# Mixer of an adaLN block: order of the copies behind a step's attention, one maximum per step, and the place of a kept copy of h

## The chip, the cores and the metric

One Trainium2 chip, one of its cores. The time is the device time of one execution in microseconds (us): the median over the runs shown. TensorE is PE here (its weight loads PEld), VectorE is DVE, ScalarE is ACT, GpSimd is POOL, and SP issues most of the DMAs.

## What is computed

The block runs an attention-and-scan stage over 16 sequences of 512 tokens of width 256, then an MLP, then a mixture of 8 experts. The change lies in the first stage, the "mixer". Cut to it:

```python
h = _layernorm(x, axis=-1) * (1 + ca) + sa          # modulated input, kept for the residual
xn = _layernorm(h, ln1_g, ln1_b)                    # second norm, of h
scores = einsum('bhncd,bhnkd->bhnck', Qb, Kw) / sqrt(Dh)
scores = where(mask, scores, -inf)                  # window of 64 queries, band of 128 keys
p = softmax(scores); o = einsum('bhnck,bhnkd->bhncd', p, Vw)
attn = o @ W_O + b_O
drive = xn @ B_w + u;  s2 = A * s + ut              # scan over the tokens
x1 = h + g * attn + (1.0 - g) * y_ssm
```

## The kernel before

The mixer is a loop over 16 batches, `body(b, last)` on each engine. The first and the last batch are written out, the 14 between them are a hardware loop. Engines are ordered by semaphores alone; each engine runs its own list in program order.

A batch begins with the projections (PE L129 to L131; the helper's lines). Then come 11 steps (`for s in steps`), a software pipeline over the 8 windows of 64 queries. In step s PE does, in this order:

- `scores_by_query(b, s)`: the scores of window s with queries on the partitions, into `sc[:, 0:2, :]` (L631, L636). They serve only to find each query's maximum.
- `scores_by_key(b, s-1)`: the scores of window s-1 again, with keys on the partitions, minus the maxima (L650, L658, L662). It waits for `maxT_sb`, the maxima turned onto a row and copied to `w["shift"]`.
- `values(b, s-2)`: probabilities times V, into `pv` (L672). It waits for `o_norm` of the window before.
- the turning of the maxima of window s (L734, into `pm`), then the turning of the normalised output of window s-3 (L744).

DVE does in step s: the two `tensor_reduce` (L887) of window s, one for each half of `sc`; in step 1 the scan (L899, L902); `layer_norms(dve, b + 1, s)`, which is a part of the two norms of the NEXT batch (step 0: statistics of x, which waits for the loads of x and of its modulation rows `shsc`; 1: aggregate; 2: normalise; 5: statistics of h; 6: aggregate; 7: normalise); then the reciprocal and the normalising of window s-2 (L908, L912), which wait for `pv_mm`; then the copy of the turned maxima (L917), which waits for `maxT_mm`; then the low half of the output (L921).

POOL refines the inverse roots of these norms by twelve small operations each (L101 to L104), computes h of the next batch (L989, L992) and the residual sum x1 (L1008). Before it overwrites `h` it waits for `h_kept`: that `h` of the batch before has been copied to `hres` by a DMA (L541).

In step 8 PE turns the next batch's normalised x (`transpose_x`, L569), which waits for step 7's normalising, and begins the output projections (`outputs`). `outputs(b, 0)` waits for all eight copies of maxima, since it writes the bank `pm` in which they are turned.

SP's list in a batch: four copies of K (L526), the load of the next x and `shsc` (L515, L520), in batch 0 alone `start.store_rest` (waits for the gates' modulation, which DVE computes in step 3 of batch 0) and `start.store_blanks` (L219, L236, L239), then the store of the gate rows to `scratch["xs"]` (L538), then the copy of h to `hres` (L541), then the store of x1 (L543).

Of the kernel before, what the change touches and what calls it, by code (L numbers as in the profile page):

```python
# [19 lines left out]
ALU = mybir.AluOpType  # L20
ACT = mybir.ActivationFunctionType
AX = mybir.AxisListType
# [11 lines left out]
WIN = 64  # L34
NW = L // WIN
# [361 lines left out]
def mixer(nc, din, w, scratch, out, NB):  # L397


    with ExitStack() as ctx:  # L400
# [68 lines left out]
        st_hi = m.counter("st_hi", 1)  # L469
        st_lo = m.counter("st_lo", 1)  # L470
        q_scores = m.counter("q_scores", 2 * NW)
        maxed = m.counter("maxed", 2 * NW)
        maxT_mm = m.counter("maxT_mm", NW)
        maxT_sb = m.counter("maxT_sb", NW)
        k_scores = m.counter("k_scores", NW)
# [32 lines left out]
        @block.sync  # L508
        def _(sp):
            def load(b):  # L510
                load_x(b)
                load_modulation(b)

            def load_x(b):
                sp.dma_start(x[:], din["x"][bass.ds(b, 1), :, :].rearrange("a (t p) d -> p (a t) d", p=P)  # L515
                             ).then_inc(x_in.sem, 16)

            def load_modulation(b):
                row = scratch["mod"][bass.ds(b, 1), 0:2 * D].rearrange("a (i d) -> a i d", i=2)
                sp.dma_start(shsc[:], row.to_broadcast([P, 2, D])).then_inc(x_in.sem, 16)  # L520

            def body(b, last):
                sp.wait_ge(k_lo.sem, k_lo.at(b, 2))
                for j in range(4):
                    r = slice(32 * j, 32 * j + 32)
                    sp.dma_start(Kz[r, j % 2, :, :, WIN:], Kt[r, :, :, :]).then_inc(k_spread.sem, 16)  # L526
                if isinstance(b, int) and b == 0:
                    start.store_bias_rows(sp)
                if not last:
                    sp.wait_ge(s_norm0.sem, s_norm0.at(b, 4))  # L530
                    sp.wait_ge(s_h.sem, s_h.at(b, 2))
                    load(b + 1)
                if isinstance(b, int) and b == 0:
                    start.store_rest(sp)
                    sp.wait_ge(start.mod_out.sem, 32)
                    start.store_blanks(sp)
                gate = scratch["mod"][bass.ds(b, 1), 5 * D:6 * D].to_broadcast([L, D])
                sp.dma_start(scratch["xs"][bass.ds(b * L, L), D:2 * D], gate).then_inc(gate_out.sem, 16)  # L538
                sp.wait_ge(s_h.sem, s_h.at(b, 2))
                sp.wait_ge(x1_sb.sem, x1_sb.at(b, 0))  # L540
                sp.dma_start(hres[:], h[:]).then_inc(h_kept.sem, 16)  # L541
                sp.wait_ge(x1_sb.sem, x1_sb.at(b, TT))
                sp.dma_start(scratch["x1"][bass.ds(b, 1), :, :].rearrange("a (t p) d -> p (a t) d", p=P),  # L543
                             x1[:]).then_inc(x1_out.sem, 16)

            load_x(0)
            start.load_job(sp, 0)
            start.load_vectors(sp)
            for j in range(1, len(start.jobs)):
                start.load_job(sp, j)  # L550
            start.store_shift_and_scale(sp)
            sp.wait_ge(start.mod_out.sem, 16)
            load_modulation(0)
            start.copy_constants(sp)
            loop(sp, body)
            sp.wait_ge(x1_out.sem, 16 * NB)
            sp.wait_ge(start.blank_out.sem, 48)
            sp.wait_ge(start.v_in.sem, 16 * 7)
            sp.wait_ge(gate_out.sem, 16 * NB)

        @block.tensor
        def _(pe):
# [59 lines left out]
            def scores_by_query(b, n):  # L622

                var = 1 if n == 0 else 0
                if n == 0:
                    pe.wait_ge(q_lo.sem, q_lo.at(b, 4))
                else:
                    pe.wait_ge(maxed.sem, maxed.at(b, 2 * n))
                for h in range(2):
                    r = half_rows(h)  # L630
                    pe.matmul(sc[:, h, :], w["twoI"][r, :], w["maskq"][r, var, :, :], start=True, stop=False)  # L631
# [74 lines left out]
            def body(b, last):  # L706
                project(b)
                for s in steps:
# [21 lines left out]
                    if 0 <= s - 2 < NW:  # L730
                        values(b, s - 2)
                    if s < NW:
                        pe.wait_ge(maxed.sem, maxed.at(b, 2 * s + 2))
                        pe.transpose(maxT, mx[:, s % 2, :], w["identb"][:]).then_inc(maxT_mm.sem, 1)  # L734
                    if s == NW + 1:
                        outputs(b, 1)
# [117 lines left out]
        def _(dve):  # L854
# [17 lines left out]
            def body(b, last):  # L872
# [9 lines left out]
                                      ).then_inc(k_lo.sem, 1)  # L882
                for s in steps:
                    if s < NW:
                        for c in range(2):
                            dve.wait_ge(q_scores.sem, q_scores.at(b, 2 * s + c + 1))
                            dve.tensor_reduce(mx[:, s % 2, WIN * c:WIN * c + 4],  # L887
                                              sc[:, c, :].rearrange("p (j k) -> p j k", j=4),
                                              AX.X, ALU.max).then_inc(maxed.sem, 1)
                    if isinstance(b, int) and b == 0 and s == 0:  # L890
                        for j in range(3, 6):
                            start.low_part(dve, j, start.low)
# [9 lines left out]
                        dve.tensor_copy(sth[:], st[:]).then_inc(st_hi.sem, 1)  # L902
                    if not last:
                        layer_norms(dve, b + 1, s)
                    if 0 <= s - 2 < NW:
                        n = s - 2
                        dve.wait_ge(pv_mm.sem, pv_mm.at(b, n + 1))
# [2 lines left out]
                        for par in range(2):  # L910
# [1 line left out]
                            dve.tensor_tensor(on[r, n % 2, :, :], pvO[r, :, DH * par:DH * par + DH],  # L912
                                              rden[r, n % 2, :].unsqueeze(2).to_broadcast([WIN, PAIRS, DH]),
                                              ALU.mult).then_inc(o_norm.sem, 1)
                    if s < NW:
                        dve.wait_ge(maxT_mm.sem, maxT_mm.at(b, s + 1))
                        dve.tensor_copy(w["shift"][:, s % 2, :], maxT).then_inc(maxT_sb.sem, 1)  # L917
                    if 0 <= s - 3 < NW:
                        n = s - 3
                        dve.wait_ge(oT_hi.sem, oT_hi.at(b, n + 1))  # L920
# [1095 lines left out]
```

## Time and profile before

| | us |
|---|---|
| median of 3 runs | 2383.28 |
| lowest and highest | 2371.1, 2385.2 |
| the profiled execution, device time | 2362.23 |
| its span, first to last instruction | 2360.1 |
| mixer: batch 0's first step to the last x1 | about 54 to 1160 |
| PE busy over the span | 1995.8 (85%) |
| DVE busy over the span | 1429.3 (61%) |
| mean granted TensorE clock | 0.898 |

The mixer takes nearly half of the span. The profiled execution is 21 us below the median of the runs shown. A timeline row gives start, duration (or the stretch that merged instructions cover), engine, line, operation, output and inputs, the count, and in brackets the idle time of the engine before it with what ended it.

### The profile page before, as it was taken

The numbers are of one execution on the slowest core, as the hardware profiler recorded it, in microseconds if no ns is written. First come the engines' busy times: TensorE is split into PE (matmuls) and PEld (weight loads), VectorE is DVE, ScalarE is ACT, GpSimd is POOL, SyncE is SP. The second block draws the span as 40 slices with busy tenths as digits, with TensorE's granted clock in tenths as the row PEclk, the third lists the DMA queues.
The fourth block names the chain that finished last, engine by engine and source line by source line (L and its number), as shares of the span: only waits on it lengthen the run. The fifth ranks groups of instructions, "written<-read, shape, count | busy, mean of one in ns | idle before, by whom it ended". The sixth has DMA issues, their size and how long they took to land. (4 is left out here: it accounts for less than half of the span.)

```text
span 2360.1 us, 58051 instructions
## 1 busy us (share of the span) xinstructions
PE 1995.8 (85%) x19628; PEld 1589.9 (67%) x19629; DVE 1429.3 (61%) x3705; ACT 961.8 (41%) x1734; POOL 993.9 (42%) x1131
## 2 busy tenths in 40 slices
PE   4488988888889888889698988888089999999997
PEld 1366767666667666667556666666078888888886
DVE  5345454555555555554378888888345566666665
ACT  3133222233333323233165444455055565656564
POOL 3121121212112212222046766777446666666664
PEclk7689797998899999998799888889589999999999
DMA  3112001111110111111144333333135444554544
GB/s 121 54 50 50 18 31 49 49 49 49 49 36 23 39 49 49 49 49 36 47 131 134 119 115 117 119 125 121 37 86 91 88 91 92 94 90 89 92 92 61
DMA packets 155521, 172.90 MB, mean 73 GB/s; under 512 B 35141, under 2 KB 136200, under 8 KB 155329
## 3 DMA queue, kind: packets, MB, share of 16 engines
q1 hardware_dynamic: 101248, 96.90, 14.9%
q0 software_dynamic: 36352, 56.78, 12.9%
q10 hardware_dynamic: 17856, 18.37, 2.2%
q8 instruction: 40, 0.66, 0.1%
q14 instruction: 25, 0.20, 0.0%
HBM read 109.40 MB, written 53.99 MB: 69 GB/s over the span
## 5 line engine op out<-in xcount | busy, mean ns | idle before, releaser
L1878 POOL DMA_INDIRECT out<-experts_y,experts_entry x144 | 237.4, 1649 | 192.9 <-DVE experts_y L1854 165.9
L672 PE MATMUL mixer_pv<-w_V,mixer_prob 128*128 128x33 f32 x2048 | 271.7, 290 | 14.3 <-DVE mixer_on L912 14.3
L672 PEld LDWEIGHTS mixer_pv<-w_V,mixer_prob 128*128 128x128 f32 x2048 | 259.1, 205 | 28.2 <-issue 19.2
L799 ACT ACTIVATE mixer_prob<-mixer_sc 128x1024 f32<-128x1024 f32 x128 | 130.9, 1023 | 236.1 <-PE mixer_sc L662 236.1
L887 DVE TENSOR_REDUCE w_mx<-mixer_sc 128x4 bf16<-128x512 f32 x256 | 163.8, 681 | 90.4 <-PE mixer_sc L636 90.4
L1819 DVE TENSOR_SCALAR experts_v<-experts_v 128x512 f32<-128x512 f32 x144 | 74.6, 518 | 218.8 <-ACT experts_v L1793 218.8
L1793 ACT ACTIVATE experts_g<-experts_pg,x_b 128x256 f32<-128x256 f32 x288 | 120.9, 471 | 183.1 <-PE experts_pv L131 183.0
L1868 POOL DMA_INDIRECT experts_rows<-scratch_xs,experts_entry x144 | 168.7, 1171 | 59.4 <-issue 42.4
L1008 POOL TENSOR_TENSOR mixer_x<-mixer_mix,mixer_hres 128x256 f32<-128x256 f32 x64 | 46.5, 726 | 333.2 <-DVE mixer_mix L868 332.2
L129 PE MATMUL experts_pg<-experts_xT,x_w 128*128 128x256 f16 x576 | 158.1, 274 | 11.3 <-issue 8.7
L908 DVE RECIPROCAL mixer_rden<-mixer_pv 128x8 f32<-128x8 f32 x128 | 26.4, 207 | 232.1 <-PE mixer_pv L672 232.1
L1493 POOL DMA_INDIRECT scratch_queue<-mlp_entry,mlp_slot x128 | 142.2, 1111 | 50.9 <-issue 38.6
L129 PE MATMUL experts_py<-x_w,experts_hh 128*128 x576 | 157.7, 274 | 2.1 <-DVE experts_hl L1831 2.1
L131 PE MATMUL experts_py<-x_w,experts_hl 128*128 x576 | 157.8, 274 | 0.0
L130 PE MATMUL experts_py<-x_w,experts_hh 128*128 x576 | 157.7, 274 | 0.0
L131 PE MATMUL experts_pg<-experts_xT,x_w 128*128 128x256 f16 x576 | 157.6, 274 | 0.0
L130 PE MATMUL experts_pg<-experts_xT,x_w 128*128 128x256 f16 x576 | 157.6, 274 | 0.0
L129 PE MATMUL experts_pv<-experts_xT,x_w 128*128 128x256 f16 x576 | 157.5, 273 | 0.0
L131 PE MATMUL experts_pv<-experts_xT,x_w 128*128 128x256 f16 x576 | 157.4, 273 | 0.0
L130 PE MATMUL experts_pv<-experts_xT,x_w 128*128 128x256 f16 x576 | 157.4, 273 | 0.0
L650 PE MATMUL mixer_sc<-w_twoI,w_maskq 64*128 64x512 bf16 x256 | 55.2, 427 | 115.4 <-DVE w_shift L917 98.0
L662 PE MATMUL mixer_sc<-mixer_Qh,w_Kz 64*128 64x128 f16 x2048 | 150.1, 236 | 0.0
(364 smaller groups left out, 6022.3 us busy)
## 6 DMA issues: line engine op xcount, KB each, us to landing
mixer_x<-in_x SPq DMA_DIRECT2D x16, 512.0 KB, 3.9
w_Kz<-mixer_Kt SPq DMA_DIRECT2D x64, 128.0 KB, 2.4
scratch_xs<-scratch_mod SPq DMA_DIRECT2D x16, 512.0 KB, 10.0
mixer_hres<-mixer_h SPq DMA_DIRECT2D x16, 512.0 KB, 10.4
scratch_x<-mixer_x SPq DMA_DIRECT2D x16, 512.0 KB, 2.9
mlp_xa<-scratch_x SPq DMA_DIRECT2D x16, 512.0 KB, 4.3
mlp_stage<-in_x_w SPq DMA_DIRECT2D x16, 512.0 KB, 4.3
mlp_xb<-scratch_x SPq DMA_DIRECT2D x16, 512.0 KB
```

What stands on the lines that cost most here:

```text
L129: pe.matmul(out, lhs[0], rhs[0], start=start, stop=False)
L130: pe.matmul(out, lhs[0], rhs[1], start=False, stop=False)
L131: return pe.matmul(out, lhs[1], rhs[0], start=False, stop=stop)
L662: last = pe.matmul(sc[:, 2 + h, at:at + P], Kz[half_rows(h), j, i, c, keys], queries(q, h, c, n), start=False, stop=(c + j == 2 and i == 1))
L672: last = pe.matmul(pvO[:, i, :], prob[:, n % 2, at:at + P], V[:, n, i, :], start=True, stop=True)
L799: act.activation(prob[:, n % 2, :].rearrange("p (c j) -> p c j", c=2), sc[:, 2:4, :], ACT.Exp, scale=SCALE).then_inc(exped.sem, 1)
L887: dve.tensor_reduce(mx[:, s % 2, WIN * c:WIN * c + 4], sc[:, c, :].rearrange("p (j k) -> p j k", j=4), AX.X, ALU.max).then_inc(maxed.sem, 1)
L1493: pool.indirect_dma_start(out=scratch["queue"], out_offset=bass.IndirectOffsetOnAxis(ap=slot[:, 2 * t + k:2 * t + k + 1], axis=0), in_=ent ...
L1793: act.activation(dst[:, q, f * ROWS:(f + 1) * ROWS], bank[:, q, f * ROWS:(f + 1) * ROWS], fn, bias=x["b1"][:, bass.ds(e, 1), bias + 2 * q ...
L1819: dve.tensor_scalar(v[:, q, :], v[:, q, :], -8.0, 10.0, ALU.max, ALU.min).then_inc(v_cut.sem, 1)
L1868: pool.indirect_dma_start(out=rows[:, s, t, :], out_offset=None, in_=scratch["xs"], in_offset=bass.IndirectOffsetOnAxis(ap=entry[:, s, t, ...
L1878: pool.indirect_dma_start(out=out, out_offset=bass.IndirectOffsetOnAxis(ap=entry[:, s, t, 0:1].bitcast(I32), axis=0), in_=y[:, s % 2, t, : ...
```

## The change

Four edits, all in the mixer.

1. One `tensor_reduce` over both halves of `sc` (128 x 1024 elements to 128 x 8) takes the place of two (128 x 512 to 128 x 4). It waits for both score counts; `maxed` counts one per step.
2. The copy of the turned maxima (L917) goes ahead of the reciprocal and the normalising. It stays behind the norms and the scan of its step.
3. On SP the copy of h to `hres` goes ahead of batch 0's start-up stores and of the gate store.
4. PE's waits on `maxed` follow the new count.

```diff
-        maxed = m.counter("maxed", 2 * NW)
+        maxed = m.counter("maxed", NW)
...
                     load(b + 1)
+                sp.wait_ge(s_h.sem, s_h.at(b, 2))
+                sp.wait_ge(x1_sb.sem, x1_sb.at(b, 0))
+                sp.dma_start(hres[:], h[:]).then_inc(h_kept.sem, 16)
                 if isinstance(b, int) and b == 0:
                     start.store_rest(sp)
                     sp.wait_ge(start.mod_out.sem, 32)
                     start.store_blanks(sp)
                 gate = scratch["mod"][bass.ds(b, 1), 5 * D:6 * D].to_broadcast([L, D])
                 sp.dma_start(scratch["xs"][bass.ds(b * L, L), D:2 * D], gate).then_inc(gate_out.sem, 16)
-                sp.wait_ge(s_h.sem, s_h.at(b, 2))
-                sp.wait_ge(x1_sb.sem, x1_sb.at(b, 0))
-                sp.dma_start(hres[:], h[:]).then_inc(h_kept.sem, 16)
...
-                    pe.wait_ge(maxed.sem, maxed.at(b, 2 * n))
+                    pe.wait_ge(maxed.sem, maxed.at(b, n))
...
-                        pe.wait_ge(maxed.sem, maxed.at(b, 2 * s + 2))
+                        pe.wait_ge(maxed.sem, maxed.at(b, s + 1))
...
-                        for c in range(2):
-                            dve.wait_ge(q_scores.sem, q_scores.at(b, 2 * s + c + 1))
-                            dve.tensor_reduce(mx[:, s % 2, WIN * c:WIN * c + 4],
-                                              sc[:, c, :].rearrange("p (j k) -> p j k", j=4),
-                                              AX.X, ALU.max).then_inc(maxed.sem, 1)
+                        dve.wait_ge(q_scores.sem, q_scores.at(b, 2 * s + 2))
+                        dve.tensor_reduce(mx[:, s % 2, :].rearrange("p (h r) -> p h r", h=2)[:, :, 0:4],
+                                          sc[:, 0:2, :].rearrange("p h (j k) -> p h j k", j=4),
+                                          AX.X, ALU.max).then_inc(maxed.sem, 1)
...
                         layer_norms(dve, b + 1, s)
+                    if s < NW:
+                        dve.wait_ge(maxT_mm.sem, maxT_mm.at(b, s + 1))
+                        dve.tensor_copy(w["shift"][:, s % 2, :], maxT).then_inc(maxT_sb.sem, 1)
                     if 0 <= s - 2 < NW:
...
-                    if s < NW:
-                        dve.wait_ge(maxT_mm.sem, maxT_mm.at(b, s + 1))
-                        dve.tensor_copy(w["shift"][:, s % 2, :], maxT).then_inc(maxT_sb.sem, 1)
                     if 0 <= s - 3 < NW:
```

## Rows read from the trace of the kernel before

**Rows 1.** The page's costliest groups: count, busy, mean ns, idle before and releaser.

```profile
L887 DVE TENSOR_REDUCE w_mx<-mixer_sc 128x4 bf16<-128x512 f32 x256 | 163.8, 681 | 90.4 <-PE mixer_sc L636 90.4
...
L650 PE MATMUL mixer_sc<-w_twoI,w_maskq 64*128 64x512 bf16 x256 | 55.2, 427 | 115.4 <-DVE w_shift L917 98.0
```

**Rows 2.** Timeline of PE, batch 9: steps 1 and 3, then step 3 into 4.

```profile
707.90 0.61 PE L650 MATMUL mixer_sc<-w_twoI,w_maskq 64*128 64x512 bf16 x2 [2.73 <-DVE w_shift L917]
...
719.80 0.39 PE L650 MATMUL mixer_sc<-w_twoI,w_maskq 64*128 64x512 bf16 x2 [0.60 <-DVE w_shift L917]
...
722.82 0.22 PE L734 MATMUL mixer_pm<-w_identb,w_mx 128*128 128x128 bf16 x1
...
723.32 0.39 PE L636 MATMUL mixer_sc<-w_Kz,mixer_Qh 64*128 64x128 f16 x8
724.19 0.39 PE L650 MATMUL mixer_sc<-w_twoI,w_maskq 64*128 64x512 bf16 x2 [0.48 <-DVE w_shift L917]
```

**Rows 3.** Timeline of PE, batch 2, at half clock: two steps without that wait.

```profile
252.99 0.64 PE L636 MATMUL mixer_sc<-w_Kz,mixer_Qh 64*128 64x128 f16 x8
253.54 0.61 PE L650 MATMUL mixer_sc<-w_twoI,w_maskq 64*128 64x512 bf16 x2
...
260.61 0.61 PE L650 MATMUL mixer_sc<-w_twoI,w_maskq 64*128 64x512 bf16 x2
```

**Rows 4.** Timeline of DVE, batch 9, steps 3 to 7.

```profile
723.02 0.21 DVE L908 RECIPROCAL mixer_rden<-mixer_pv 128x8 f32<-128x8 f32 x1 [2.09 <-PE mixer_pv L672]
...
723.91 0.23 DVE L917 COPY w_shift<-mixer_pm 128x128 bf16<-128x128 bf16 x1
...
724.37 1.28 DVE L887 TENSOR_REDUCE w_mx<-mixer_sc 128x4 bf16<-128x512 f32 x2
...
729.96 1.39 DVE L820 BATCH_NORM_STATS2 mixer_stats<-mixer_h 128x6 f32<-128x256 f32 x4
...
733.15 1.28 DVE L887 TENSOR_REDUCE w_mx<-mixer_sc 128x4 bf16<-128x512 f32 x2
...
735.15 0.17 DVE L94 TENSOR_SCALAR mixer_rs<-mixer_rs 128x4 int32<-128x4 int32 x1
...
739.85 1.38 DVE L832 TENSOR_SCALAR mixer_nrm<-mixer_h,mixer_mv,mixer_rs 128x256 f32<-128x256 f32 x4 [1.03 <-POOL mixer_rs L104]
```

**Rows 5.** Timeline of PE, batch 9, start of step 8.

```profile
741.36 1.59 PE L569 MATMUL mixer_sc<-w_identf,mixer_nrm 128*128 128x128 f32 x8 [0.65 <-DVE mixer_nrm L832]
```

**Rows 6.** Timeline of SP, batch 0: its DMA issues.

```profile
57.25 0.51 SPq L520 DMA_DIRECT2D mixer_shsc<-scratch_mod  x1
79.14 0.34 SPq L219 DMA_DIRECT2D scratch_mod<-setup_mod  x1
...
89.69 11.54 SPq L541 DMA_DIRECT2D mixer_hres<-mixer_h  x1
```

**Rows 7.** The same batch on POOL, DVE and PE.

```profile
108.38 2.34 POOL L989 TENSOR_TENSOR mixer_h<-mixer_nrm,mixer_shsc 128x1024 f32<-128x1024 f32 x1 [36.11 <-DMA mixer_hres<-mixer_h]
...
113.17 1.40 DVE L820 BATCH_NORM_STATS2 mixer_stats<-mixer_h 128x6 f32<-128x256 f32 x4 [24.46 <-POOL mixer_h L992]
...
115.64 0.61 PE L650 MATMUL mixer_sc<-w_twoI,w_maskq 64*128 64x512 bf16 x2 [23.30 <-DVE w_shift L917]
...
126.49 1.04 PE L569 MATMUL mixer_sc<-w_identf,mixer_nrm 128*128 128x128 f32 x8
```

**Rows 8.** Timeline of PE, last batch, start of step 8.

```profile
1142.52 0.27 PE L129 MATMUL mixer_pm<-w_c_hi,mixer_sth 128*128 128x256 f16 x1 [1.12 <-DVE w_shift L917]
```

**Rows 9.** DMA issues of 700 to 716 us: count, KB, us to landing.

```profile
mixer_hres<-mixer_h SPq DMA_DIRECT2D x1, 512.0 KB, 10.6
mixer_shsc<-scratch_mod SPq DMA_DIRECT2D x1, 256.0 KB, 4.9
```

**Rows 10.** Stretches: length, busy time and count of each engine, PEclk, DMA share, GB/s.

```profile
741.00:747.00 6.00, 5.64 (x58) 4.47 (x58) 1.44 (x6) 2.80 (x6) 0.00 (x0) 0.72 0.00 0
246.00:270.00 24.00, 23.52 (x199) 20.15 (x193) 11.70 (x40) 6.12 (x10) 2.38 (x12) 0.52 0.00 0
```

## Prediction

> **What bounds the kernel now.** I read the page first: how busy each engine is, the granted clock along the span, and the costliest groups. In the mixer the slices show PE at 80 to 90%, with DVE at half and ACT and POOL below, so PE sets the pace and what counts is the time it stands. The group of L650, the first matmul of `scores_by_key`, is where it stands: 98.0 us of idle time, all released by the copy of the maxima, L917 [rows 1]. The list of PE's waits gives 87 such waits. The timeline of PE sorts them. In batch 0 one is 23.30 us [rows 7]. Step 1 of each later batch waits 1.7 to 3.2 us (2.73 in [rows 2]; 7.5 in batch 0). Step 3 waits 0.60 and steps 4 to 7 wait 0.48 each [rows 2], wherever PE is at full clock. At half clock there is no wait: L650 follows the scores at once [rows 3].
>
> The timeline of DVE says why. In step 3 the reciprocal starts at 723.02, when the values are done; the copy comes last at 723.91, though PE had turned the maxima at 722.82 + 0.22 = 723.04 [rows 2, 4]. PE stands until 724.19 for a copy of 0.23 us that two other operations delay by 0.89 us.
>
> **The copy ahead of the normalising.** DVE stands idle for 1.8 to 2.1 us before the values of steps 3 and 4 end [rows 4], so it is free when the turned maxima come. The copy then runs from about 723.09 to 723.32. Before, L650 started 0.05 after the copy's end (724.14, 724.19), so it could go at 723.37. PE's own order lets it go later: the modelled end of the last score matmul is 724.19 - 0.48 = 723.71, and at half clock L650 starts 0.09 before that modelled end (252.99 + 0.64 = 253.63, start 253.54) [rows 3]. At full clock I take 0.06, hence 723.65. The gain is 0.48 + 0.06 = 0.54 us in a step and 0.60 + 0.06 = 0.66 in step 3; the bounds are 0.48 and 0.6 for the one, 0.60 and 0.7 for the other. The period of a step goes from 4.39 (719.80 to 724.19) to 3.85.
>
> What is behind the copy on DVE? The reciprocal starts 0.3 us later and the reduction only 0.05 later (724.42), since the same operations have changed places. PE asks for the normalised output only a step later. The maxima of that reduction are wanted at the next turning, 722.16 + 3.85 = 726.0; they are there at 725.7 at the latest. Nothing new waits there.
>
> Step 5 is tighter. Its statistics of h end at 729.96 + 1.39 = 731.35 [rows 4] and move with the turning of step 4, by 0.66 + 0.54 = 1.20, to about 730.1. The turning of step 5 (731.60, two periods behind 722.82) moves by 1.74 to 729.86, and the copy could start at 730.13. That is a tie: the full gain stays, with nothing to spare.
>
> Steps 6 and 7 gain nothing in a batch that prepares the next one. The seed of the second root ends at 735.15 + 0.17, POOL's twelve steps bring the normalising to 739.85, and PE turns the result at 741.36 after a wait of 0.65 [rows 4, 5]. That chain, 6.0 us, has no part in this change. It hangs on the reduction of step 6 (733.15), so on the turning of step 5. PE arrives 0.54 + 0.54 earlier and stands 1.7 instead of 0.65. The gain of a middle batch is therefore 0.66 + 0.54 + 0.54 = 1.74 us, and 14 batches give **24.4 us**. Step 1 stays as it is: the copy stays behind the statistics that wait for the load, and step 2's wait is for ACT.
>
> The last batch has no norms. Steps 3, 6 and 7 gain 0.66 + 2 x 0.54 (its steps 4 and 5 run at half clock, without a wait). The wait of 1.12 before its output projections [rows 8] loses the same 0.85 by which the copy comes earlier. Together **2.6 us**.
>
> **One reduction for two.** Two of 0.681 us cover 1.28 [rows 1, 4]. The joint one lies between 0.68 and 1.36; I take 1.20, near the upper end since every element is still read once. It is hidden behind PE by half a microsecond or more in steps 2 to 7, and in step 0 the load is later anyway. At 0.08 us in 16 last reductions at most it is 1 us; I take 0. The Trainium skill, "VectorE: DVE Perf Modes", section "The TRN2 errata", says that one large tile pays the fixed cost once and many small ones pay it each; its formula would make it an estimated 1.19 us. It agrees with the value from the rows and changes nothing.
>
> **h kept first.** In batch 0 POOL stands 36.11 us for the copy of h [rows 7]. It is issued only at 89.69, behind the start-up stores, which wait for DVE's step 3 and begin at 79.14; even its issue takes 11.54 us in the full queue [rows 6]. POOL's h comes at 113.1, DVE's statistics of step 5 wait 24.46 us for it, the copy of step 5 is behind these, and PE stands 23.30 us [rows 7]. With the edit the copy is issued at 57.8, behind the load of 57.25. Its own wait, for x1 of the batch before, is no wait in batch 0. Landing takes 10.6 us beside a gate store of equal size [rows 9], so it lands by 68.4, before POOL asks at 108.38 - 36.11 = 72.3. What was late goes: 23.3 us. The copies of steps 3 and 4 give 0.66 + 0.54. Then the next limit: from L650 to the turned x was 126.49 - 115.64 = 10.85 at half clock; at full clock it is 741.36 - (724.19 + 2 x 4.39) = 8.4, and 8.9 with PE 0.54 earlier. Of these 1.9 us I count all, since PE comes without a stand. Together **26.4 us**. The blanks and the gate store inherit the full queue, until some 101 us; the next SP work, the copies of K, comes after 120, so nobody waits.
>
> In the other batches the copy of h lands earlier, which nobody asks for: POOL's h waits for the normalising there. The gate store has no reader in the mixer.
>
> **The sum.** 24.4 + 2.6 + 26.4 = 53.4 us. Against the profiled execution, 2362.2, that is 2308.8. The median of the runs shown is 2383.3, 21 us above it, and the measurement is of medians, so I forecast **2330 us**, 2.2% less. Its own range: 12 us either way for half a period's errors in 14 batches and the spread of runs, 2316 to 2344.
>
> **Rivals.**
>
> The clock helps. In batch 2 the granted clock is 0.52 over 246 to 270 [rows 10], after steps with 0.48 us waits; there a step takes 260.61 - 253.54 = 7.07 us, 2.68 more than at full clock [rows 3]. Three such passages, in batches 2, 4 and 15, of about three steps each cost 24 us. If PE without its small waits keeps the clock, they go: 2306. The Trainium skill, "TensorE: Matmul & The Clock Gate", section "A second HAM failure mode: psum-queue depth-cycling", says that small idle gaps between groups of matmuls make the clock swing and that the way back is paid each time. By it the waits of steps 3 to 7 would be what starts these passages; the trace bears it only so far, since most batches have the same waits and no passage.
>
> The clock hurts. The change gathers idle time in front of L569, 1.7 instead of 0.65. In batch 9 the clock fell there: 0.72 over 741 to 747, so 6 x 0.28 = 1.7 us lost [rows 10]. About nine batches keep their clock there now; if all fall, 15 us come back: 2345.
>
> The start-up stall stays, because h or its space is held by something else. For it: two waits of the same kind sit on POOL. Against: the row names the DMA alone. Then 26 us fail: 2356.
>
> The copies bring nothing in the middle batches, because the next wait (values, probabilities, statistics in step 5) takes their place. For it: the tie in step 5. Against: DVE's 1.8 us idle time and the exponentials, which end well before PE asks. Then 24 us fail: 2354.
>
> Slower. The copy of h now follows the load directly, and both move through the same queue. Step 1 waits for `shsc`, landing 4.9 us after its issue [rows 9], and each microsecond later is one on PE, 15 times. Half of the 10.6 us that both stores take is 5.3, the most that could come in front: 80 us, so 2330 + 80 = 2410. It decides from 53 / 15 = 3.5 us on. Against: the load is issued first, and today the gate store follows it as closely.
>
> **Chances.** The forecast 0.52; the clock helps 0.20; it hurts 0.10; the stall stays 0.05; no gain in the middle 0.08; slower 0.03; the rest, a gain under 1%, 0.02. The range from 2298 to 2356 takes in both clock rivals, with the spread of the runs before (12 us below the median) in part, and reaches both failed halves. A measurement of this kernel tells about 1% from no change, so faster means below 2359.4: 0.92 of the cases less some spread, 0.90; within 1% 0.07; slower 0.03.
>
> **What would show it.** Right: one wait of 36 us on POOL gone and h copied from about 58 us; L650's idle time down from 98.0 to about 38 us, nearly all of it step 1; step 3 to 5 periods of 3.85; the wait before L569 at about 1.7; L887 at 128 times 1.2 us. Wrong: waits of L650 in steps 4 and 5, a new wait on L672 or L631, `shsc` landing after 6 us or more, or PEclk below 0.85 in the mixer after 100 us. The forecast is wrong above all if the clock's passages move, as each is worth 8 us.

## The result, and the profile after

The changed kernel takes **2291.35 us** (median of 4 runs, 2284.92 to 2295.01). The kernel before, on the same chip, takes 2383.22 us (2371.10 to 2385.20). The ratio is 0.9622, with the interval 0.9583 to 0.9660. That is 3.8% faster, and 6.6 us below the low end of the forecast range. The profiled execution took 2284.92 us (span 2282.8, mean granted clock 0.907) against 2362.23 us (span 2360.1, clock 0.898) before: 77.3 us less.

The page's groups that answer to [rows 1] and to [rows 9] (count, busy us, mean ns, then idle time before and what ended it):

```profile
L886 DVE TENSOR_REDUCE w_mx<-mixer_sc 128x8 bf16<-128x1024 f32 x128 | 156.0, 1219 | 92.1 <-PE mixer_sc L636 91.6
...
mixer_hres<-mixer_h SPq DMA_DIRECT2D x16, 512.0 KB, 4.8
```

One reduction takes 1.219 us; two took 2 x 0.681. The copy of h lands 4.8 us after its issue in the median, where the page of before has 10.4, since the gate store no longer goes first (e2, which moves this copy alone, has 4.8 too).

The changed kernel's list of PE's waits over batches 0 to 14 (61 to 1050 us): us in total, times, the longest.

```profile
PE mixer_sc L650 <- DVE w_shift L906: 34.6, 16, 7.7
PE mixer_sc L569 <- DVE mixer_nrm L832: 27.8, 15, 2.0
```

L650 waited 87 times for the copy of the maxima before, now 16 times: once in step 1 of each of batches 0 to 14, and in batch 0 once more (step 4, 2.59 us). The wait before L569 stands in each batch that prepares a next one. The timeline of PE shows it, with a whole batch between the first two rows and then steps 1 to 4 and 8 of one:

```profile
643.14 0.39 PE L631 MATMUL mixer_sc<-w_maskq,w_twoI 64*128 64x512 bf16 x2 [0.43 <-DMA w_Kz<-mixer_Kt]
...
647.98 0.61 PE L650 MATMUL mixer_sc<-w_twoI,w_maskq 64*128 64x512 bf16 x2 [1.68 <-DVE w_shift L906]
...
654.53 0.39 PE L650 MATMUL mixer_sc<-w_twoI,w_maskq 64*128 64x512 bf16 x2 [1.09 <-ACT mixer_prob L799]
...
659.59 0.38 PE L650 MATMUL mixer_sc<-w_twoI,w_maskq 64*128 64x512 bf16 x2
...
663.32 0.38 PE L650 MATMUL mixer_sc<-w_twoI,w_maskq 64*128 64x512 bf16 x2
...
679.70 1.97 PE L569 MATMUL mixer_sc<-w_identf,mixer_nrm 128*128 128x128 f32 x8 [1.85 <-DVE mixer_nrm L832]
...
707.99 0.39 PE L631 MATMUL mixer_sc<-w_maskq,w_twoI 64*128 64x512 bf16 x2 [0.38 <-DMA w_Kz<-mixer_Kt]
```

Steps 3 and 4 have no bracket any more, where [rows 2] had 0.60 and 0.48. A step takes 663.32 - 659.59 = 3.73 us (4.39 before). L569 stands 1.85 us and then runs for 1.97 us. At full clock, as in batch 0 (at 100.54), it takes 1.09.

Where did 77.3 us go? Three marks in the two profiled executions split them. They are PE's first score matmul (L631) of batch 1 and of batch 14, and the MLP's first turning. First the kernel before, then the changed one:

```profile
155.16 0.39 PE L631 MATMUL mixer_sc<-w_maskq,w_twoI 64*128 64x512 bf16 x2 [0.22 <-DMA w_Kz<-mixer_Kt]
...
1034.12 0.39 PE L631 MATMUL mixer_sc<-w_maskq,w_twoI 64*128 64x512 bf16 x2 [0.41 <-DMA w_Kz<-mixer_Kt]
...
1173.78 1.97 PE L1168 MATMUL mlp_pj<-w_identf,mlp_nrm 128*128 128x128 f32 x8 [15.10 <-DVE mlp_nrm L1348]
```

```profile
127.23 0.39 PE L631 MATMUL mixer_sc<-w_maskq,w_twoI 64*128 64x512 bf16 x2 [0.23 <-DMA w_Kz<-mixer_Kt]
...
967.43 0.39 PE L631 MATMUL mixer_sc<-w_maskq,w_twoI 64*128 64x512 bf16 x2 [0.41 <-DMA w_Kz<-mixer_Kt]
...
1094.17 1.97 PE L1167 MATMUL mlp_pj<-w_identf,mlp_nrm 128*128 128x128 f32 x8 [15.00 <-DVE mlp_nrm L1347]
```

| part | measured gain | forecast |
|---|---|---|
| up to batch 1 (155.16 to 127.23) | 27.9 | 26.4 |
| 13 middle batches (879.0 long, now 840.2) | 38.8 | 13 x 1.74 = 22.6 |
| batch 14 and the last (139.7, now 126.7) | 12.9 | 1.74 + 2.6 = 4.3 |
| MLP and experts | -2.3 | 0 |

The parts in excess, 16.2 and 8.6 us, are in the main the three half-clock passages of the forecast's first rival. In the kernel before, they held nine groups of 16 value matmuls (L672) that took 3.6 us instead of 1.97: three each in batch 2, batch 4 and the last. The six in the middle batches, at 7.07 - 4.39 = 2.68 us each [rows 3], are 16.1 us. In the last batch the L650 of steps 3 to 6 start 7.04, 7.06 and 5.79 us apart instead of 4.39, which is 6.7 of its 8.6 us. One such group of the kernel before:

```profile
248.72 3.62 PE L672 MATMUL mixer_pv<-w_V,mixer_prob 128*128 128x33 f32 x16
```

The profiled execution of before has 11 of them: at 82 and 118, at 249 to 263, at 389 to 403, at 1116 and 1123, and at 1148 us. The changed kernel's has two, at 82 and 1069, and none in batches 1 to 14.

### The profile page after: what moved, and what is told of

Read it like the earlier page. It is cut to its first block and busy times, and to the rows that moved or that the text cites. A ratio compares the mean times of both kernels' runs of the same rounds, so it can differ in the third digit from the quotient of the medians.

```text
span 2282.8 us, 57727 instructions
## 1 busy us (share of the span) xinstructions
PE 1963.1 (86%) x19628; PEld 1571.1 (69%) x19629; DVE 1416.2 (62%) x3577; ACT 964.0 (42%) x1734; POOL 995.2 (44%) x1131
## 5 line engine op out<-in xcount | busy, mean ns | idle before, releaser
L672 PE MATMUL mixer_pv<-w_V,mixer_prob 128*128 128x33 f32 x2048 | 254.3, 280 | 13.0 <-DVE mixer_on L914 13.0
L672 PEld LDWEIGHTS mixer_pv<-w_V,mixer_prob 128*128 128x128 f32 x2048 | 241.7, 194 | 26.3 <-DVE mixer_on L914 13.9
L886 DVE TENSOR_REDUCE w_mx<-mixer_sc 128x8 bf16<-128x1024 f32 x128 | 156.0, 1219 | 92.1 <-PE mixer_sc L636 91.6
L129 PE MATMUL mlp_po<-w_w_hi,mlp_hidh 128*128 128x256 f16 x512 | 144.2, 282 | 1.0 <-issue 0.7
L130 PE MATMUL mlp_po<-w_w_lo,mlp_hidh 128*128 128x256 f16 x512 | 143.3, 280 | 0.0
L131 PE MATMUL mlp_po<-w_w_hi,mlp_hidl 128*128 128x256 f16 x512 | 143.2, 280 | 0.0
```

Source lines behind the costliest of these rows:

```text
L129: pe.matmul(out, lhs[0], rhs[0], start=start, stop=False)
L130: pe.matmul(out, lhs[0], rhs[1], start=False, stop=False)
L131: return pe.matmul(out, lhs[1], rhs[0], start=False, stop=stop)
L672: last = pe.matmul(pvO[:, i, :], prob[:, n % 2, at:at + P], V[:, n, i, :], start=True, stop=True)
L886: dve.tensor_reduce(mx[:, s % 2, :].rearrange("p (h r) -> p h r", h=2)[:, :, 0:4], sc[:, 0:2, :].rearrange("p h (j k) -> p h j k", j=4), A ...
```

## The experiments

All variants are derived from one of the two kernels and compute the same result. Kernels sent together ran on the same chip and share the runs of the kernel before, whose median was 2393.46 us in the first set (e1 to e4), 2383.98 in the second (e5 to e8) and 2385.06 in the third (e9 to e11). Where kernels of different sets are compared below, the sets' medians differ by up to 10 us. "Half-clock groups" are the groups of 16 value matmuls, out of 128, that took over 3.2 us in the profiled execution.

**Which part carries the gain.** Each of the three parts alone, put into the kernel before.

e1, the copy alone:

```diff
                         layer_norms(dve, b + 1, s)
+                    if s < NW:
+                        dve.wait_ge(maxT_mm.sem, maxT_mm.at(b, s + 1))
+                        dve.tensor_copy(w["shift"][:, s % 2, :], maxT).then_inc(maxT_sb.sem, 1)
...
-                    if s < NW:
-                        dve.wait_ge(maxT_mm.sem, maxT_mm.at(b, s + 1))
-                        dve.tensor_copy(w["shift"][:, s % 2, :], maxT).then_inc(maxT_sb.sem, 1)
```

> The kernel before with one edit: the copy of the turned maxima ahead of the reciprocal and the normalising. Theory (the excess over the forecast is half-clock passages in the steps, set off by the short waits of L650, and the copy's move alone removes them): the steps' 24.4 us and the last batch's 2.6 us, plus 25 to 38 us of passages that go, so 2383 - 27 - 32 = 2324 us, between 2315 and 2332; no stretch of several steps at half clock in batches 1 to 14; POOL's 36 us wait for the kept copy of h stays. Rival (the passages come from the start-up stall, or their going is chance or the work of the other edits): 2383 - 27 = 2356 us, with passages still there.

Measured: 2322.23 us, ratio 0.9705 (0.9645 to 0.9765), so 71 us, within the range of this run's theory. Its waits removed are worth 24.4 + 2.6 = 27.0 by the forecast's own count. 6 half-clock groups; the two in the middle batches (at 459 and 722 us) are single ones and come behind L569, as the last values of their batch.

e2, the copy of h alone:

```diff
                     load(b + 1)
+                sp.wait_ge(s_h.sem, s_h.at(b, 2))
+                sp.wait_ge(x1_sb.sem, x1_sb.at(b, 0))
+                sp.dma_start(hres[:], h[:]).then_inc(h_kept.sem, 16)
...
-                sp.wait_ge(s_h.sem, s_h.at(b, 2))
-                sp.wait_ge(x1_sb.sem, x1_sb.at(b, 0))
-                sp.dma_start(hres[:], h[:]).then_inc(h_kept.sem, 16)
```

> The kernel before with one edit: on SP the copy of h goes ahead of the start-up stores and the gate store. Theory: only the start-up stall goes, 25 us (23.3 of the stand, about 2 of what follows), so 2358 us; the waits of L650 in steps 3 to 7 stay at 0.48 to 0.60 and half-clock passages stay, two to five of them. Rival (the stall sets off the passages later, so they go with it): 2358 - 32 = 2326 us.

Measured: 2364.91 us, ratio 0.9878 (0.9838 to 0.9917), 28.6 us, the forecast's 26.4 within the interval. Of passages this run's expectation had two to five in view; its profile holds 19 half-clock groups, 18 of them in seven passages of batches 1 to 14.

e3, the joint maximum alone:

```diff
-                        for c in range(2):
-                            dve.wait_ge(q_scores.sem, q_scores.at(b, 2 * s + c + 1))
-                            dve.tensor_reduce(...).then_inc(maxed.sem, 1)
+                        dve.wait_ge(q_scores.sem, q_scores.at(b, 2 * s + 2))
+                        dve.tensor_reduce(...).then_inc(maxed.sem, 1)
```

> The kernel before with one edit: one maximum operation for two. Theory: the operation is 1.22 us for 1.28 and hidden, so no difference, within 2 us of before, and the waits of L650 unchanged. Rival (the shorter operation and the joint wait shift the steps and thereby the clock): a difference of 8 us or a multiple, with passages gone or new.

Measured: 2385.25 us, ratio 0.9973 (0.9934 to 1.0011): no difference that can be measured.

So the copy is 71 us and h 29. Together 100, against 92 for all of the change (this set's runs of the kernel before are 10 us longer). The start-up part was sized rightly; the copy was 44 us too small. These profiles show where to look. The windows view over 180 to 1000 us (busy time of PE, PEld, DVE, ACT, POOL, then the granted clock), first of the kernel before, then of e2, then of e3:

```profile
180.00:1000.00 820.00, 712.56 (x8055) 560.76 (x8054) 456.68 (x1266) 248.26 (x399) 162.24 (x372) 0.90 0.16 42
```

```profile
180.00:1000.00 820.00, 726.67 (x7774) 572.85 (x7772) 442.84 (x1223) 241.16 (x387) 160.95 (x365) 0.85 0.16 42
```

```profile
180.00:1000.00 820.00, 725.09 (x7741) 572.49 (x7741) 436.47 (x1133) 241.25 (x389) 154.63 (x358) 0.86 0.16 42
```

e2 and e3 leave the waits of steps 3 to 7 as they are, and have **19 and 23** half-clock groups, against 11 in the profile that the forecast rested on. e3's profiled span is 2390.8 us against 2360.1; twelve groups at 2.68 us each, 32 us, account for these 31 us. The runs of the kernel before beside them tell the same with time and mean clock alone: eighteen of them go from 2376.12 us at 0.892 to 2410.38 us at 0.874, nearly in order. The profile of before (2362.23 at 0.898) is faster than any other run of that kernel seen here; it caught few passages.

**Does the wait itself set off the passages?** e4 takes the idle time away without taking the wait away. Four extra matmuls, whose result is overwritten unread, fill PE's time before L650's wait in steps 3 to 7 of the kernel before. The wait for the exponentials, which frees the bank they write, stands ahead of them.

```diff
+            def busy(count):
+                for _ in range(count):
+                    pe.matmul(sc[:, 2, 0:240], w["identh"][:], xTh[:, 0, 0:240], start=True, stop=True)
...
+                if 2 <= n < NW - 1:
+                    busy(4)
                 pe.wait_ge(maxT_sb.sem, maxT_sb.at(b, n + 1))
```

> The kernel before, with PE given something to do in the short waits: four matmuls of 240 columns, whose result is overwritten, ahead of L650's wait in steps 3 to 7 (each about 0.1 us at full clock, 0.4 us in all, against waits of 0.48 and 0.60). Nothing else moves. Theory (the short idle times set off the half-clock passages): the passages go though work is added, 2383 - 32 = about 2351 us, and a granted clock above 0.93 over batches 1 to 14. Rival (the idle times have no part in it; what decides is how dense the steps' own matmuls are, or chance): no gain, and where a passage is, each step in it gets 0.8 us longer, so 2383 to 2395 us.

Measured: 2346.48 us (2341.16 to 2350.56), ratio 0.9811 (0.9747 to 0.9876). Its timeline of PE in batch 2, where the kernel before was at half clock:

```profile
246.35 0.39 PE L656 MATMUL mixer_sc<-w_twoI,w_maskq 64*128 64x512 bf16 x2
...
247.56 1.97 PE L678 MATMUL mixer_pv<-w_V,mixer_prob 128*128 128x33 f32 x16
...
250.18 0.58 PE L644 MATMUL mixer_sc<-w_xTh,w_identh 128*128 128x240 f16 x4
250.74 0.39 PE L656 MATMUL mixer_sc<-w_twoI,w_maskq 64*128 64x512 bf16 x2
```

The step is as long as before, 250.74 - 246.35 = 4.39 us: the copy comes no sooner. Two half-clock groups are left, at 117 and 134 us, both in batch 0. The granted clock over 180 to 1000 us is 0.92, where the expectation wanted over 0.93. PE does 320 more matmuls and the kernel is 47 us faster. The 17 and 21 groups fewer than in e2 and e3, at 2.68 us, are 46 and 56 us. This is the size of the 44 us that e1 gained beyond its waits, brought about without moving the copy.

e11 is the same with `busy(2)` in place of `busy(4)`, so that part of the idle time stays.

> The kernel before, with two instead of four matmuls of 240 columns in the short waits, so that about 0.27 us of each stays idle. Theory (as above): no passages, as with four, 2346 to 2356 us. Rival (the passages go only when nothing of the wait is left idle): several passages, 2365 to 2390 us.

Measured: 2338.08 us (2335.29 to 2339.94), ratio 0.9813 (0.9749 to 0.9878), 8 us below the range expected. 3 half-clock groups, none in batches 1 to 14. Two matmuls were enough:

```profile
251.83 0.39 PE L656 MATMUL mixer_sc<-w_twoI,w_maskq 64*128 64x512 bf16 x2 [0.17 <-DVE w_shift L923]
```

A wait of 0.29 us in step 3 and of 0.17 us in steps 4 to 7 brings no passages back.

**The other way round: put the wait back into the changed kernel.** e8 and e9 leave DVE's order as changed and put a `memset` of an unused tile ahead of the copy in four steps, 640 elements in e8 and 960 in e9.

```diff
                         dve.wait_ge(maxT_mm.sem, maxT_mm.at(b, s + 1))
+                        if s in (2, 3, 4, 6):
+                            dve.memset(idle[:], 0.0)
                         dve.tensor_copy(w["shift"][:, s % 2, :], maxT).then_inc(maxT_sb.sem, 1)
```

> The kernel after, with a filling of 640 elements (about 0.7 us, nobody reads it) put on DVE ahead of the copy in steps 2, 3, 4 and 6. It brings back a wait of L650 of about 0.5 us in three or four steps of a batch, with everything else as in after. Theory (short idle times in the steps set off half-clock passages): beside the 14 x 3 x 0.5 = 20 us of waits, passages come back, two to six of about 8 us, so 2291 + 20 + 16 to 48 = 2327 to 2360 us, and value groups of 3.62 us in batches 1 to 14. Rival (the passages went with the order of the operations or by chance): 2291 + 20 = 2311 us, no such group.

Measured: 2291.15 us (2290.63 to 2300.70), ratio 0.9614 (0.9569 to 0.9658), 1 half-clock group. The waits before L650 came back at 0.27 to 0.38 us, shorter than the 0.48 that was aimed at, and no passage came. Nor did the 20 us that both sides had put down for the waits: a batch lasts 64.86 us in the mean, against 64.66. As a test of the 0.48 us it is inconclusive, so it was followed by e9.

> The kernel after, with the filling on DVE ahead of the copy made longer, 960 elements instead of 640, so that the wait of L650 in four steps of a batch is about 0.5 us, as in before, instead of 0.27 (all the rest as in after). Theory (waits of that length set off the half-clock passages, shorter ones don't): passages come back, value groups of 3.62 us in batches 1 to 14, and the time goes to 2330 to 2365 us. Rival (no dependence on the waits' length; the passages belong to the order of before or to chance): no such groups, 2291 to 2305 us.

Measured: **2405.53 us** (2395.64 to 2416.08), ratio 1.0115 (1.0045 to 1.0186), 1.2% slower than the kernel before and 40 us above the range expected. 21 half-clock groups. Timeline of PE in e8, then in e9 (line numbers are one higher than in the changed kernel):

```profile
227.25 0.39 PE L651 MATMUL mixer_sc<-w_twoI,w_maskq 64*128 64x512 bf16 x2 [0.27 <-DVE w_shift L909]
228.46 1.97 PE L673 MATMUL mixer_pv<-w_V,mixer_prob 128*128 128x33 f32 x16
```

```profile
228.43 0.39 PE L651 MATMUL mixer_sc<-w_twoI,w_maskq 64*128 64x512 bf16 x2 [0.60 <-DVE w_shift L909]
229.64 1.97 PE L673 MATMUL mixer_pv<-w_V,mixer_prob 128*128 128x33 f32 x16
...
232.93 0.59 PE L651 MATMUL mixer_sc<-w_twoI,w_maskq 64*128 64x512 bf16 x2 [0.60 <-DVE w_shift L909]
...
235.15 3.62 PE L673 MATMUL mixer_pv<-w_V,mixer_prob 128*128 128x33 f32 x16
...
242.12 3.62 PE L673 MATMUL mixer_pv<-w_V,mixer_prob 128*128 128x33 f32 x16
...
249.36 3.62 PE L673 MATMUL mixer_pv<-w_V,mixer_prob 128*128 128x33 f32 x16
```

In this batch of e9 three steps with waits of 0.72, 0.60 and 0.60 us are followed by three steps at half clock; 12 of batches 1 to 14 have one to three such steps there. The windows view of the same stretch of e9, and of 180 to 1000 us, shows the clock (0.50, and 0.83 over all); e8's stands beneath:

```profile
180.00:1000.00 820.00, 722.98 (x7534) 571.00 (x7532) 450.02 (x1139) 235.52 (x381) 152.76 (x346) 0.83 0.15 42
234.00:252.00 18.00, 17.92 (x161) 15.52 (x155) 9.86 (x29) 3.60 (x5) 2.39 (x12) 0.50 0.00 0
```

```profile
180.00:1000.00 820.00, 718.78 (x8360) 564.39 (x8358) 483.70 (x1256) 259.60 (x417) 173.16 (x391) 0.92 0.17 46
```

Four waits in each of 16 batches, some 0.33 us longer (0.60 against 0.27), make at most 21 us, and the wait before L569 gives most of it back (1.48 us in e8, 0.22 in most batches of e9). The kernel is 114 us slower. The rest goes with the clock: over 180 to 1000 us alone, (0.92 - 0.83) x 820 = 74 us of full speed are missing. No matmul was added or taken away between e8 and e9, so the number of PE's own matmuls, which e4 and e11 change, is not what decides here. The waits of e9 are somewhat longer than the 0.48 to 0.60 us of the kernel before, so e9 shows the dependence and not that 0.48 us are enough; for that there are only before, e2 and e3 against e4 and e11.

**Does the wait before L569 cost clock?** The rival "the clock hurts" priced L569's fall to half clock at 15 us. e5 fills that wait of the changed kernel with 14 of the same extra matmuls, unread again.

```diff
                         if not last:
+                            pe.wait_ge(exped.sem, exped.at(b, NW - 1))
+                            busy(14)
                             transpose_x(b + 1)
```

> The kernel after, with fourteen matmuls of 240 columns (0.1 us each at full clock, result overwritten) ahead of the wait for step 7's normalising, where PE now stands 1.85 us in each batch and L569 then starts at half clock. Theory (that idle time lowers the clock there, and the lower clock costs 1.5 us a batch): the turns of x run at full clock, 1.09 instead of 1.97 us, the outputs behind them too, and the kernel gains 14 x 1.2 to 1.7 = 17 to 24 us over after, 2291 - 20 = 2271 us. Rival (the clock falls there for another reason, or what it costs is hidden): 2291 us or up to 5 more.

Measured: 2289.46 us (2285.95 to 2291.68), ratio 0.9588 (0.9548 to 0.9629): the changed kernel's time. The groups by form over 61 to 1050 us (count, busy, mean ns, idle before) of the changed kernel and of e5:

```profile
L569 PE MATMUL mixer_sc<-w_identf,mixer_nrm 128*128 128x128 f32 x120 | 28.0, 409 | 27.8 <-DVE mixer_nrm L832 27.8
```

```profile
L569 PE MATMUL mixer_sc<-w_identf,mixer_nrm 128*128 128x128 f32 x120 | 16.3, 279 | 5.9 <-DVE mixer_nrm L838 5.9
```

L569 runs at full clock in e5, as wanted, and nothing is gained. The windows view says why. The changed kernel, from L569 on, and then e5 in the same places of its batch:

```profile
678.00:683.00 5.00, 3.30 (x16) 2.86 (x17) 2.50 (x9) 2.23 (x5) 0.15 (x1) 0.66 0.00 0
683.00:688.00 5.00, 4.20 (x60) 3.53 (x58) 1.03 (x5) 1.80 (x3) 0.00 (x0) 1.00 0.00 0
688.00:693.00 5.00, 5.00 (x33) 4.09 (x33) 2.04 (x6) 0.26 (x1) 0.00 (x0) 0.67 0.00 0
```

```profile
684.00:688.00 4.00, 3.60 (x34) 2.96 (x34) 2.47 (x9) 1.82 (x3) 0.00 (x0) 1.00 0.00 0
689.00:694.00 5.00, 4.20 (x35) 3.90 (x29) 2.28 (x6) 1.29 (x2) 0.00 (x0) 0.81 0.00 0
694.00:699.00 5.00, 5.00 (x25) 4.00 (x26) 0.82 (x4) 0.27 (x1) 0.00 (x0) 0.50 0.00 0
```

The half-clock stretch has moved from L569 to the last values and the output projections. e5 has 15 half-clock groups. Thirteen are one in each of batches 2 to 14, that batch's last values. They cost no time against the changed kernel, which has two groups in all: the count stands for lost time only where a whole step is stretched, as in steps 3 to 7. A batch takes 707.99 - 643.14 = 64.85 us in the changed kernel and 713.88 - 649.04 = 64.84 in e5. The expected gain is refuted; what the clock costs behind step 8 is not set by the wait before L569 alone.

**Removing the cause of that wait.** Steps 6 and 7 gain nothing since the chain of the second norm (statistics, root, normalising) hangs on step 6. e6 starts it a step earlier in the changed kernel.

```diff
-            if part == 5:
+            if part == 4:
                 dve.wait_ge(s_h.sem, s_h.at(b, 2))
                 moments(dve, b, h, 1)
-            if part == 6:
+            if part == 5:
                 aggregate(dve, b, 1)
```

> The kernel after, with the statistics of h in step 4 instead of 5 and their aggregate in step 5 instead of 6; the normalising stays in step 7. Theory (the chain from the aggregate over POOL's twelve operations to the normalising is what ends PE's wait of 1.85 us before L569): the root is ready before step 7, the wait falls to about 0.15 us, and with the full clock kept there 14 x (1.7 + 1.2) = 41 us go, at the least 14 x 1.7 = 24: 2250 to 2267 us. Rival (DVE in step 7, the reduction and the normalising, is as late as the root): the wait stays above 1 us and the time above 2280.

Measured: 2243.20 us (2241.36 to 2248.03), ratio 0.9401 (0.9360 to 0.9443), 7 us below the range expected. That is 48 us below the changed kernel, 3.4 us in each of 14 batches, where the wait is 1.85. The same group in e6:

```profile
L569 PE MATMUL mixer_sc<-w_identf,mixer_nrm 128*128 128x128 f32 x120 | 16.3, 279 | 0.8
```

The wait is gone, L569 keeps full clock, and the granted clock over 180 to 1000 us is 0.93 against 0.90. The marks inside a batch, as means over batches 1 to 13, place the gain: from L650 of step 2 to L569 25.18 us in the changed kernel and 23.38 in e6, 1.80 less; from L569 to the next batch's L650 of step 1 32.99 and 31.56, 1.43 less. In that second stretch of one batch the granted clock is 0.86 in the changed kernel (679.70 to 712.67) and 0.90 in e6 (595.59 to 627.18). So the remaining 1.5 us lie where the clock is higher; that the clock is all of their cause is argued, not shown. The forecast's reading of that chain, that it alone sets PE's end of steps 6 and 7, is confirmed.

e7 adds to e6 the copy ahead of the statistics in step 0, against the wait in step 1.

```diff
+                    if s == 0:
+                        dve.wait_ge(maxT_mm.sem, maxT_mm.at(b, s + 1))
+                        dve.tensor_copy(w["shift"][:, s % 2, :], maxT).then_inc(maxT_sb.sem, 1)
                     if not last:
                         layer_norms(dve, b + 1, s)
-                    if s < NW:
+                    if 0 < s < NW:
```

> As the one before, and in step 0 the copy of the maxima goes ahead of the statistics of x, which wait for the load. Theory (step 1's wait of L650, 1.5 to 2.2 us, is for that copy alone): the wait goes, but the reduction of step 1 stands behind the same load and the copy of step 1 behind the scan, so about 0.5 to 1 us a batch is left of it: 2240 to 2262 us, 8 to 14 under the kernel without this edit. Rival (the chain of DVE in step 1 takes all of it back): no difference from the kernel without this edit.

Measured: 2247.58 us (2239.72 to 2253.93), ratio 0.9407 (0.9359 to 0.9456): no gain over e6, as its rival said, though the time lies in the range of the theory. The wait has moved one step on, behind the scan and the aggregate:

```profile
632.33 0.64 PE L650 MATMUL mixer_sc<-w_twoI,w_maskq 64*128 64x512 bf16 x2
...
638.81 0.39 PE L650 MATMUL mixer_sc<-w_twoI,w_maskq 64*128 64x512 bf16 x2 [1.42 <-DVE w_shift L909]
```

Step 1 has no wait, step 2 has 1.42 us. There are 15 half-clock groups against 2 in e6, four of them in batch 0.

e10 goes from e6 to ACT instead, which ends the 1.09 us wait of step 2: the exponentials go ahead of the gates' tanh.

```diff
+                    if 0 <= s - 1 < NW:
+                        n = s - 1
+                        act.wait_ge(k_scores.sem, k_scores.at(b, n + 1))
+                        act.activation(..., ACT.Exp, scale=SCALE).then_inc(exped.sem, 1)
                     if s in (1, 2):
...
-                    if 0 <= s - 1 < NW:
-                        n = s - 1
-                        act.wait_ge(k_scores.sem, k_scores.at(b, n + 1))
-                        act.activation(..., ACT.Exp, scale=SCALE).then_inc(exped.sem, 1)
```

> The kernel with the norms of h one step earlier, and on ACT in steps 1 and 2 the exponential ahead of the gates' tanh. Theory (step 2's wait of L650, 1.09 us in each batch, is for an exponential that stands behind the tanh and the gate matmuls): that wait goes or falls to what the copy of step 1 needs, 0.5 to 1 us a batch, so 2228 to 2236 us against 2243. Rival (what is saved in a batch is taken by the clock elsewhere in it, as in the kernel with matmuls before the turn): no difference from 2243, and the batch still lasts 61.5 us.

Measured: **2226.44 us** (2225.52 to 2227.36), ratio 0.9348 (0.9287 to 0.9410), the fastest version here: 65 us below the changed kernel, 17 below e6 (of another set), and 2 below the range expected. 7 half-clock groups. Its timeline, the L650 of steps 1 and 2:

```profile
619.46 0.39 PE L650 MATMUL mixer_sc<-w_twoI,w_maskq 64*128 64x512 bf16 x2 [1.97 <-DVE w_shift L906]
...
624.42 0.38 PE L650 MATMUL mixer_sc<-w_twoI,w_maskq 64*128 64x512 bf16 x2
```

## Why the prediction was wrong, step by step

The waits went where the forecast said. One term of its sum failed, the clock's, and one agreement is luck.

- **Steps 3 to 7.** The waits of L650 in them are gone. From L650 in step 1 to L569 a batch took 741.36 - 707.90 = 33.46 us [rows 2, 5] and takes 679.70 - 647.98 = 31.72: 1.74 us less, the forecast to the digit, and that is luck. A step is 3.73 us long, not 3.85, so each gains 0.66 instead of 0.54, and the first of them 0.77 instead of 0.66; the wait before L569, 1.85 and not 1.7, takes a part. Between L650 of step 2 and L569 a batch thus gained 27.40 - 25.18 = 2.22 us in the mean. In this pair of batches step 1 took 0.48 back (6.07 and 6.55 us, at a granted clock of 0.74 and 0.68). The floor was taken from a half-clock start plus a margin; the real overlap is 0.12 us larger.
- **Step 5's tie** held: no wait of L650 behind it.
- **The root chain** absorbs steps 6 and 7: confirmed in place by the wait of 1.85, and by e6, which moves the chain and takes the wait away.
- **Start-up.** 27.9 us measured, 28.6 in e2, 26.4 forecast. POOL's 36 us wait for the copy of h is gone. The copy is issued at 56.99 us (57.8 forecast).
- **The joint reduction** costs nothing (e3), at 1.219 us where 1.20 was taken. The Trainium skill, "VectorE: DVE Perf Modes", section "The TRN2 errata", gave an estimated 1.19; the trace is 2% above.
- **`shsc`** lands 4.1 us after its issue in the median (4.0 before; the 4.9 of [rows 9] is one issue), so the slower rival had no part.
- **A sum.** The chances of a gain over 1% add up to 0.52 + 0.20 + 0.10 + 0.05 + 0.08 = 0.95, not 0.92.

What failed is one term: **the clock's passages**, which the sum held at zero and put aside as a rival of 24 us with a chance of 0.20. Two errors lie in it.

First, the cause. The forecast let the passages stand since most batches have the same waits and no passage. That a cause acts only in some batches does not clear it. e4 and e11 take the idle time away and leave every wait's end where it was: the passages go, and with them 47 and 47 us. e9 puts 0.6 to 0.7 us back: passages in 12 of 14 batches, where e8, with 0.27 to 0.38 us, has none. The waits of steps 3 to 7 set them off. Why a given batch has one and the next, with the same waits, has none stays open. The rule cited in the forecast from the Trainium skill ("TensorE: Matmul & The Clock Gate", section "A second HAM failure mode: psum-queue depth-cycling"), that small idle gaps make the clock swing and the way back is paid each time, agrees with these runs (granted clock 0.92 in e8, 0.83 in e9).

Second, the size. 24 us was three passages counted in the one profiled execution. That execution was 21 us below the median of the others, and the forecast carried the 21 us over to the changed kernel as if it were a constant. By the profiles at hand it was made of passages: 11 half-clock groups there, 19 and 23 in the profiles of e2 and e3. The changed kernel's profiled execution lies 6.4 us below its median. So the miss of 2330 - 2291.35 = 38.7 us is 2308.8 - 2284.9 = 23.9 us, nearly all of it the passages of the profile (16.1 + 6.7), and 21.1 - 6.4 = 14.7 us, put down to those that the profile did not hold; no profile of a usual run of the kernel before was taken, so this second part rests on e2 and e3. The rival's own 2306 failed by the second part too.

The other clock rival, "it hurts", saw the fall rightly: L569 now runs at half clock in the middle batches (mean 409 ns, 279 at full clock). Its price of 15 us counted nine batches that keep their clock there, but in the trace of before only five of the 14 middle L569 groups take 1.09 us; seven take 1.29 to 1.60 us, between that and the 1.97 of half clock, so the fall was partly there already. Measured from L650 of step 1 to the next, the 11 middle batches of before without a passage last 66.44 us in the mean (65.0 to 68.1) and the 13 of the changed kernel 64.66, so 1.78 less. Of the 2.22 us won ahead of L569 the stretch from L569 to the next step 1 gives 0.50 back (32.49 and 32.99 us). That is some 7 us in 14 batches: the rival was there at half its price, hidden by steps that gained more than forecast. e5 shows that holding L569 at full clock gains nothing, as the low stretch then falls on the output projections.

## What to carry to other kernels

When PE has a short wait in each step of a loop, price it by more than its length. By the length of the path these waits were worth 1.74 us a batch, 27 us in all, and removing them was worth 71 us (e1), since PE also kept its clock; cheap extra matmuls in the gap won 47 us without shortening anything. Before a sum is made against one profiled execution, compare it with the spread of the runs: one that is faster than all of them holds fewer half-clock passages than usual, and the difference is itself a term of the sum. And follow the chain that takes over: the wait that the change left before L569 was worth another 48 us.

## What the runs showed of the hardware

- **A small step in the wait tips the clock.** In steps of 3.7 to 4.5 us full of small matmuls, waits of 0.17 to 0.29 us (e11) and of 0.27 to 0.38 us (e8) left 3 and 1 half-clock groups, none in a step of batches 1 to 14. Waits of 0.48 to 0.60 us (before, e2, e3) gave 11, 19 and 23, and 0.60 to 0.72 us (e9) gave 21 and a granted clock of 0.83 over 180 to 1000 us. Where between them it turns was not measured, nor whether it is the same in a step with other work.
- **A batch keeps its length while its contents change.** The changed kernel and e5 have batches of 64.85 and 64.84 us, though one runs L569 at half clock and the other at full clock with 14 more matmuls. e8, with waits in four steps and L569 at full clock, has 64.86 in the mean of 13 batches and the same total time (2291.15). It spends 1.5 us more ahead of L569 (26.70 against 25.18) and 1.4 less behind it (31.55 against 32.99). What one part saves, the low stretch takes in another. Why it comes out so equal stays open. e6, which takes the idle time before L569 away rather than filling it, broke it downwards (61.50 us), e9 upwards (71.40).
- **Time and mean granted clock go together from run to run.** The kernel before took 2376.12 us at 0.892 and 2410.38 at 0.874, with 16 runs nearly in order between. This holds for runs of one kernel only: the changed kernel and e5 both have 0.907, with 2 and 15 half-clock groups.
